# Sixteen-image Swin and frequency-gate kernel: attention values by token, 64x64 transform tiles, and a new order of the late slots

## The reference, cut to what matters

```python
# block 1: window attention (8x8 windows, 8 heads of 16 channels), then an MLP
t = _ln(tok).reshape(windows of 64 tokens)
q, k, v = t @ qkv_w.T + qkv_b
attn = softmax((q * scale) @ k + bias, axis=-1)     # per window and head, 64x64
tok = tok + (attn @ v) @ proj_w.T + proj_b
tok = tok + gelu(_ln(tok) @ w1.T + b1) @ w2.T + b2
# block 2: convolutions and a frequency gate
out0 = gelu(conv1x1(tok))                            # "act"
x_sca = x_att2 * abs(out0 * x_att)
x_sca = abs(ifft2(x1 * fft2(x2) * (1 + boost * mask))) * alpha + x_sca * beta   # x1, x2: 1x1 convs of x_sca
h_out, v_out = 7-tap dilated rows / columns of out0, then a 3x3 depthwise convolution each
pyr = four dilated 3x3 convolutions of out0, then a 3x3 depthwise convolution
out = relu(x + mix of h_out, v_out, pyr, out0, x_sca, gated by edge(out0))
return conv1x1(out)
```

## Time and profile before

| | us |
|---|---|
| median of 3 runs (1521.01 to 1527.33) | 1524.92 |
| the profiled execution, its device time | 1529.35 |
| its span, first to last instruction | 1527.6 |
| busy PE / DVE / ACT / POOL in the span | 1404.7 / 1321.4 / 955.9 / 408.7 |
| share of DVE in the chain that ended last, with its queue | 59% |
| share of PE / ACT in that chain | 16% / 15% |

### The profile page before, as it was taken

The page is one execution under the profiler, slowest core; times in us unless marked ns, Lnnn a source line. Parts: engine busy times, 40 slices in busy tenths (PEclk is TensorE's granted clock), DMA queues, the critical chain, the costliest instruction groups (busy, mean ns, idle before and its releaser), DMA issues.

```text
span 1527.6 us, 37499 instructions
## 1 busy us (share of the span) xinstructions
PE 1404.7 (92%) x14384; PEld 847.3 (55%) x14384; DVE 1321.4 (87%) x2312; ACT 955.9 (63%) x1717; POOL 408.7 (27%) x316
## 2 busy tenths in 40 slices
PE   5679999999999999999999999999999999999984
PEld 3346656465565646556564655656465565746552
DVE  4628898989989899998989989898989989898867
ACT  3364856667575666757566675756658575674633
POOL 3005050320505023050502305051230604024060
PEclk9789999999999999999999999999999999999997
DMA  4102012130201213020121302012130211212020
GB/s 164 26 14 67 13 33 72 17 89 15 64 29 35 72 17 89 15 64 29 32 76 17 89 15 64 29 32 76 17 89 14 54 40 32 62 17 76 1 64 28
DMA packets 32604, 70.65 MB, mean 46 GB/s; under 512 B 14116, under 2 KB 17188, under 8 KB 32068
## 3 DMA queue, kind: packets, MB, share of 16 engines
q1 hardware_dynamic: 32452, 68.28, 17.7%
HBM read 22.41 MB, written 9.08 MB: 21 GB/s over the span
## 4 chain that ended last, share of the span: by engine, by line
DVE 42%; DVEq 17%; PE 16%; ACT 15%; issue 8%; SPq 2%; DMA 1%; ACTq 0%
DVE hv L1189 15%; ACT fft L1502 6%; DVEq L1060 5%; DVE row_max L1061 4%; PE bank L743 4%; DVEq L1072 3%; DVE score L1063 3%; PE bank L547 2%; DVE inverse L1071 2%; PE bank L610 2%; ACT nT L1488 2%; ACT probT L1545 2%; ACT fft L1662 2%; DVEq L1106 2%; DVE score L1058 1%
## 5 line engine op out<-in xcount | busy, mean ns | idle before, releaser
L743 PE MATMUL bank<-act,mats_sb 128*32 128x512 f32 (+16 forms) x2592 | 221.0, 430 | 0.0
L1189 DVE SCALAR_TENSOR_TENSOR hv<-ver,mix,hv 128x1024 f32<-128x1024 f32 x144 | 184.9, 1284 | 10.8
L1875 POOL TENSOR_TENSOR resT<-qC,proj_shift 128x1024 f32<-128x1024 f32 x16 | 38.0, 2378 | 527.7 <-DVE x1T L1081 522.5
L1189 DVE SCALAR_TENSOR_TENSOR hv<-hor,mix,hv 128x1024 f32<-128x1024 f32 x128 | 164.4, 1285 | 10.9
L506 PE MATMUL bank<-cons_sb,fft 128*128 128x128 f32 x1280 | 161.1, 279 | 11.3 <-ACT fft L1502 10.1
L1502 ACT ACTIVATE fft<-bank 128x512 f32<-128x512 f32 x224 | 162.6, 802 | 12.2 <-PE bank L506 7.4
L506 PEld LDWEIGHTS bank<-cons_sb,fft 128*128 128x128 f32 x1280 | 148.8, 192 | 23.2 <-ACT fft L1502 14.3
L1895 POOL TENSOR_SCALAR hor<-act,cols_sb 128x1024 f32<-128x1024 f32 x16 | 25.0, 1565 | 488.3 <-ACT act L1579 426.3
L743 PEld LDWEIGHTS bank<-act,mats_sb 128*32 128x32 f32 x2592 | 125.5, 111 | 50.5 <-issue 30.2
L547 PE MATMUL bank<-k_heads,qC 128*64 128x512 f32 x512 | 142.0, 634 | 10.2 <-DMA k_heads<-kC 8.4
L1540 ACT ACTIVATE score<-score 128x512 f32<-128x512 f32 x128 | 80.1, 632 | 109.6 <-DVE score L1063 108.9
(11 more groups left out here) (184 smaller groups left out, 2690.8 us busy)
## 6 DMA issues: line engine op xcount, KB each, us to landing
pyr_stack<-pyr SPq DMA_DIRECT2D x96, 144.2 KB, 2.5
x_in<-x_dram SPq DMA_DIRECT2D x16, 512.0 KB, 4.9
k_heads<-kC SPq DMA_DIRECT2D x128, 64.0 KB, 2.5
edge<-edge_dram SPq DMA_DIRECT2D x16, 512.0 KB, 4.1
out_dram<-y_out SPq DMA_DIRECT2D x16, 512.0 KB, 3.4
k_heads<-rel_dram SPq DMA_DIRECT2D x2, 1024.0 KB, 13.2
mats_sb<-mats_dram SPq DMA_DIRECT2D x1, 1978.5 KB, 7.3
pyr_stack<-pyr SPq DMA_DIRECT2D x16, 123.2 KB, 2.3
```

The costliest lines, as they stand in the source:

```text
L743: last = pe.matmul(to, w_pyr[:, d, t], act[:, y0 + dy:y1 + dy, x0 + dx:x1 + dx], start=(t == 4), stop=(t == PYR_ORDER[8]), skip_group_chec ...
L1189: last = dve.scalar_tensor_tensor(hv[:], src, mix[:, a, k:k + 1], hv[:], ALU.mult, ALU.add)
```

## The change

- **Token values.** `values` swaps its operands: the probabilities are the stationary side, and `v_pair` (now with a column of ones for each head) is the moving side, so that tokens are in the partitions and each head's sum of exponentials is one column more. The four matmuls with "pair" go. DVE's reciprocal has 128x8 elements. Its product goes into a new tile `attn_tok`; a new `value_turn` on PE transposes it back to channels and a new `value_copy` on ACT puts it into `attn_out` in the natural token order.
- **64x64 tiles.** `multiply_tiles` takes the place of `multiply4` in `dft_rows`, `inverse_even`, `inverse_odd`, `last_even`, `last_odd`: 32 matmuls of 64 rows, 64 columns and 64 moved elements where there were eight of 128, without the zero blocks.
- **Tokens turned in the front.** `to_windows` and `xw` go; PE transposes `x_in` after `scores(i, 1)` and ACT copies it to an `xT` of its own. `n_copy` makes the window order instead (four pieces for two), and `swin_out` writes one piece for two. `norm1_stats` of f moves to slots 1 and 2.
- **The chain in the slots** moves to later places (`dft_rows` late in 2, `turn_spectrum` and `r_even` late in 3, `dft_columns` early in 4, `inverse_even` late in 5, `inverse_odd` and `turn_even` late in 6, `turn_odd` and `last_even` late in 7). `inverse_odd_copy` and `turn_odd_copy` go from ACT to DVE.
- **Order after the slots.** The first `pyramid_conv` stands ahead of `project(i, 1)`, `n2_transposes(i, 1)` after three `up`s; the taps are placed anew; `residual_stats(i, 0)` stands in slot 7 ahead of `scale_values(i, 7)`.

```diff
-        SLOT_TAPS = (1, 1, 1, 1, 1, 1, 1, 2, 3, 3, 5)
+        SLOT_TAPS = (1,1,1,1,1,1,1,2,2,4,6)
...
+            def multiply_tiles(first_bank, src, weights, done, first=None):
+
+                pe.sem_inc(pe_turns)
+                for c in range(CH):
+                    for q in range(2):
+                        part = slice(64 * q, 64 * q + 64)
+                        rhs = (first if first is not None and c == 0 else weights)[part, part]
+                        for m in range(2):
+                            last = pe.matmul(bank[first_bank + q][64 * m:64 * m + 64, 64 * c:64 * c + 64],
+                                             src[part, c * P + 64 * m:c * P + 64 * m + 64], rhs, start=True, stop=True)
+                        if c == CH - 1:
+                            last.then_inc(done, 1)
...
             def values(i, j):
                 pe.wait_ge(pT_sb, 8 * i + j + 1)
                 if j >= 2:
-                    pe.wait_ge(o_scaled, 8 * i + j - 1)
+                    pe.wait_ge(oT_sb, 8 * i + j - 1)
                 ps = bank[(1, 3)[j % 2]]
...
+                        last = pe.matmul(ps[64 * e:64 * e + 64, VW * g:VW * g + VW],
+                                         probT[:, j % 2, g, e * WT:(e + 1) * WT],
+                                         v_pair[:, 2 * j + e, g].rearrange("p e d -> p (e d)"), start=True, stop=True)
...
+            def value_turn(i, j):
+                pe.wait_ge(o_scaled, 8 * i + j + 1)
+                pe.transpose(bank[(1, 3)[j % 2]][:, 3 * P:4 * P], attn_tok[:, j % 2], ident).then_inc(oT_ps, 1)
...
+                ps = bank[(1, 3)[j % 2]][:, 0:HP * VW].rearrange("p (h d) -> p h d", d=HD + 1)
+                dve.reciprocal(inverse[:, j % 2], ps[:, :, HD])
...
             def both(n, i, f, late):                     # PE
                 scores(i, 0)
                 in_conv(n, i + 1)
                 scores(i, 1)
+                if f is not None:
+                    x_transposes(f, 0, 0)
+                    x_transposes(f, 1, 1)
...
-                if f is not None:
-                    next_turns(i, f, 1)
+                value_turn(i, 6)
                 last_odd(n)
+                value_turn(i, 7)
+                pyramid_conv(n, 0)
                 project(i, 1)
-                pyramid_conv(n, 0)
+                n2_transposes(i, 0)
                 pyramid_conv(n, 1)
-                n2_transposes(i, 0)
-                n2_transposes(i, 1)
                 mlp(i, n, f)
...
                 for j in range(PAIRS):                   # ACT, both
-                    conv_early(n, j)
+                    if j == 2:
+                        edge_tanh(n)
                     prob_copy(i, j)
+                    if j >= 2:
+                        value_copy(i, j - 2)
                     if j == 0 and late is not None:
                         out_copy(late)
+                    if j in (4, 5):
+                        exponent(i, j + 2)
+                    if j == 0:
+                        pyr_copy(n, 0)
                     conv_late(n, j)
...
-                    if j + 2 < PAIRS:
+                    if j < 4:
                         exponent(i, j + 2)
...
+                    elif j == 6:                         # DVE, both
+                        inverse_odd_copy(n)
+                    elif j == 7:
+                        residual_stats(i, 0)
```

More of the change, by code:

```diff
@@ L77 @@
     ("ident", P), ("dft_h", P), ("dft_w0", P), ("dft_w", P), ("even0", P),
-    ("even", P), ("odd0", P), ("odd", P), ("idft_h", P), ("high", CH), ("iota", 2), ("pair", 2 * HD))
+    ("even", P), ("odd0", P), ("odd", P), ("idft_h", P), ("high", CH), ("iota", 2))
 def shape_constants():
@@ L645, in value @@
                     v(f, k, 6 + k)
-                for t in range(6):
+                for t in range(3):
+                    up(i, t)
+                n2_transposes(i, 1)
+                for t in range(3, 6):
                     up(i, t)
@@ L918, in both @@
                     conv_late(n, j)
-                    if j == 6 and f is not None:
-                        next_turns(i, f, 0)
-                    elif j == 7:
-                        project(i, 0, f)
+                    if j == 6:
+                        project(i, 0)
                     if j == 1:
@@ L1323, in both @@
                 for j in range(1, PAIRS):
-                    if j in (4, 5):
-                        conv_slot(n, j)
+                    if j == 7:
+                        turn_odd_copy(n)
                     scale_values(i, j - 1)
+                    if j in (1, 2) and f is not None:
+                        norm1_stats(f, j - 1)
                     if j == 1:
                         mix_input(n)
-                    elif j == 3:
-                        r_even_bias(n)
+                    elif j == 4:
+                        boosted(n)
+                        even_product(n)
+                    elif j == 5:
+                        odd_product(n)
                     if j + 2 < PAIRS:
@@ L1336, in both @@
                         mix_magnitudes(n)
+                    elif j == 3:
+                        r_even_bias(n)
+                    elif j == 6:
+                        inverse_odd_copy(n)
+                    elif j == 7:
+                        residual_stats(i, 0)
                     taps(n, range(SLOT_TAPS[j], SLOT_TAPS[j + 1]))
[L1338 to L1339 removed]
                 scale_values(i, 7)
[L1341 removed]
                 norm2(i, 0)
@@ L1508, in n_copy @@
                 act_.wait_ge(nT_ps, 2 * i + k + 1)
-                copy(half(nC1, k), bank[b][:]).then_inc(nC_sb, 1)
+                for a in range(2):
+                    last = act_.activation(windows(nC1, 2 * k + a),
+                                           bank[b][:, 256 * a:256 * a + 256].rearrange("p (r b s) -> p b r s", r=WS, b=4),
+                                           ACT.Copy)
+                last.then_inc(nC_sb, 1)
             def n2_copy(i, k):
@@ L1630, in swin_out @@
                 act_.wait_ge(pyramid_mixed, i)
-                for a in range(2):
-                    last = act_.activation(natural_windows(xm[:], 2 * k + a), windows(bank[(0, 3)[k]][:], a),
-                                           ACT.Identity, bias=col("b2"))
-                last.then_inc(xm_sb, 1)
+                act_.activation(half(xm, k), bank[(0, 3)[k]][:], ACT.Identity, bias=col("b2")).then_inc(xm_sb, 1)
             def pyr_copy(n, k):
@@ L1694, in turn_even_copy @@
                     copy(half(fc, k), bank[6 + k][:]).then_inc(te_sb, 1)
-            def turn_odd_copy(n):
-                for k in range(2):
-                    act_.wait_ge(to_ps, 2 * n + k + 1)
-                    copy(half(fd, k), bank[4 + k][:]).then_inc(to_sb, 1)
             def square_even(n):
@@ L1859, in _ @@
             pool.memset(v_pair[:], 0.0)
+            pool.drain()
+            for e in range(2):
+                pool.memset(v_pair[64 * e:64 * e + 64, :, :, e, HD:HD + 1], 1.0)
+            pool.drain()
             pool.wait_ge(onehot_ready, 4)
```

238 lines of the change are left out of this document (112 added, 126 removed).

## The result

The changed kernel takes **1540.84 us** (median of 7 runs, 1533.37 to 1542.9) against 1524.92 (1520.79 to 1528.57): the ratio is 1.010, with a 95% interval of 1.0081 to 1.0119. It is slower by 1%. The changed kernel's profiled execution took 1542.9 us with a span of 1540.7; the one of before had a span of 1527.6.

What follows compares the result with a forecast made beforehand. The prediction took DVE and PE as two bounds 0.8 us apart; +0.3 us an image over 14 loop images made +4, the ends summed to 0, so 1529 us against 1524.92, with a range of 1500 to 1550.

Runs made afterwards that it cites:

- e5: The changed kernel with ACT's n2_copy(i, 1) ahead of magnitude and the gelu table load: 1555.82 us, ratio 1.027.
- e11: e10 with n2_transposes(1) ahead of all up products, behind pyramid_conv(1), and n2_copy(1) ahead of the table load: 1486.62 us, ratio 0.976.
- e3: The changed kernel with the 128x128 products of before in place of the 64x64 tiles: 1556.52 us, ratio 1.023.
- e4: The changed kernel with the exponent of pair 7 behind ACT's two copies of the even inverse: 1516.42 us, ratio 0.995.
- e6: The kernel before with the token values alone, in the old order with 128x128 transforms: 1529.35 us, ratio 1.003.
- e7: The kernel before with the token values and the five Fourier products in 64x64 tiles, in the old order: 1538.31 us, ratio 1.010.
- e8: The kernel before with the five Fourier products in 64x64 tiles alone: 1529.94 us, ratio 1.004.
- e1: The kernel before with only DVE's reciprocal cut to 8 of 128 columns (output not correctly divided): 1480.29 us, ratio 0.975.
- e2: The changed kernel with project(i, 1) ahead of the first pyramid_conv and two taps moved behind norm2(i, 1): 1537.0 us, ratio 1.013.
- e9: The changed kernel with the edits of e4 and e2 and the order of before around the second norm: 1499.52 us, ratio 0.984.
- e10: e9 with the ends of before: norm1_stats behind residual_stats(0) in swin_rest, odd copies on ACT in conv_only: 1495.08 us, ratio 0.980.
- e12: e11 with value_turn(j-2) ahead of the scores of its slot and value_copy(j-2) ahead of prob_copy: 1487.05 us, ratio 0.974.

## What to carry to other kernels

Work saved on the busiest engine is worth what the next one leaves: count each new instruction on that next engine (here eight small transposes, 2 us), and take its slack from its idle time over a whole period, not from one hand-over. If after a change both engines wait, here 5 us of 89 each, and nothing is faster, the order is the thing to look at: list the waits of one period by length, and look on each queue for an instruction that waits while what others need stands behind it. An edit that pays nothing alone can still pay beside others, since the wait may just move to the next such instruction: an earlier `n2_copy(1)` didn't pay in e5, and did in e11, where its transpose stood earlier too.

## What the runs showed of the hardware

- **The clock falls within a loop that is 93% busy.** The granted clock stays at 1.00 for images on end, and falls to half for some 3 us behind a single wait of PE. From the first loop image to 3 us behind the last, before has 6 such falls, after 6, e3 6, e4 5, e5 10, e6 2, e7 7 and e8 4. All of these 46 begin within 2 us of the end of a wait of 1.77 to 2.16 us. In e6 just two images have a wait of that length (2.13 and 2.15 us), and its two falls stand behind them. e1, e2, e9, e10, e11 and e12, whose longest wait there is 0.7 to 1.5 us, have none. But of the 96 waits of 1.7 to 2.2 us in the 14 kernels 50 have no fall behind them, and nothing here shows what decides. It is a relation, with no experiment that changes a wait and nothing else. The Trainium skill ("TensorE: Matmul & The Clock Gate", Part 1: The HAM clock gate) says that the clock is either full or half, 2.4 or 1.2 GHz; by that rule the traces agree, 4.46 us and 2.84 being one stretch mostly at the one and one at the other.
- **A tiny operation of DVE that takes six times its time.** The operation L1057 with 128x8 elements (L1038 before) took 0.17 us in the loop of before. In all 14 loop images of after it took 0.98 to 1.00 us, since it now stands beside an addition of POOL; here that ran from 714.64 to 717.01 us. First DVE, then POOL:

```profile
716.04 1.00 DVE L1057 SCALAR_TENSOR_TENSOR shift<-mv,rstd 128x8 f32<-128x8 f32 x1
```
```profile
714.64 2.37 POOL L1930 TENSOR_TENSOR resT<-xT,proj_shift 128x1024 f32<-128x1024 f32 x1 [33.36 <-DVE x1T L1102]
```

  Both have two inputs in SBUF, and the small one ends with the large one. The Trainium skill ("SBUF — State Buffer", SBUF: two separate sides) says that VectorE and GpSimd share a pair of ports, which whoever starts first holds for its whole instruction; by that rule the trace agrees.
- **A reciprocal of fewer elements is shorter, though not in proportion.** 128x128 took 0.95 us, 128x8 from PSUM 0.20. A copy from PSUM that writes with a stride took DVE 0.95 us for 128x512 (two in 1.90), a plain one 0.65 (two in 1.29).
